# 98 units of an edge network move from a graph kernel's second layer to its third

## What is computed

```
x = norm(x + L0(x))   # softmax attention over edges
x = norm(x + L1(x))   # mean over neighbours, dense layer
x = norm(x + L2(x))   # convolution: per edge h = silu(attr10 @ W_fc1 / sqrt(10)), w = h @ W_fc2 / sqrt(100)
x = norm(x + L3(x))   # per edge w_ij = mlp(edge_feats) + mlp(chi), q * w_ij * k, weighted v
mlp(x) = silu(x @ w0 + b0) @ w1 + b1       # hidden size 256
L1: nbr_sum = segment_sum(x[row], col); aggregated = nbr_sum / clip(deg, 1)
```

## Time and profile before

| | |
|---|---|
| median of 3 runs | 8727.64 us (8727.42 to 8731.45) |
| the profiled execution | 8728.76 us, of which span 8726.9 us |
| busy: TensorE, VectorE, ScalarE, GpSimd | 83%, 69%, 60%, 38% of the span |
| mean granted TensorE clock | 0.926 of full speed |

### The profile page before, as it was taken

How to read it: one execution, slowest core, us unless ns; L and a number is a source line. 1 busy time by engine, 2 the same in 40 slices (tenths; PEclk the granted TensorE clock), 3 DMA queues, 4 the chain that set the end, 5 groups by cost and what they waited for, 6 DMA issues and landing times. The chain is left out here.

```text
span 8726.9 us, 195704 instructions
## 1 busy us (share of the span) xinstructions
PE 7226.3 (83%) x51013; PEld 5596.3 (64%) x51014; DVE 6060.3 (69%) x12581; ACT 5246.3 (60%) x9329; POOL 3328.1 (38%) x3274
## 2 busy tenths in 40 slices
PE   5999999978859999999777777777778888887775
PEld 3665666667758888888555555556556666666554
DVE  7988988989983333333666666666667777777777
ACT  3666666678856666666444444444457777776553
POOL 0000000000000000000577777777747777777776
PEclk8999999999989999999888888888889999999896
DMA  3333333366644444442222222222236666666665
GB/s 110 140 134 136 138 137 137 138 213 224 226 136 133 133 133 133 132 133 92 66 54 54 54 54 54 54 54 54 54 115 206 207 208 203 207 207 197 195 196 157
DMA packets 629186, 1179.06 MB, mean 135 GB/s; under 512 B 215307, under 2 KB 289340, under 8 KB 609685
## 3 DMA queue, kind: packets, MB, share of 16 engines
q1 hardware_dynamic: 499834, 860.28, 30.4%
q0 software_dynamic: 129280, 317.93, 13.0%
HBM read 901.19 MB, written 276.57 MB: 135 GB/s over the span
## 5 line engine op out<-in xcount | busy, mean ns | idle before, releaser
L2270 POOL DMA_INDIRECT att_kv_rows<-kv_dram,att_stage x1616 | 1624.8, 1005 | 594.8 <-issue 487.5
L2025 POOL DMA_INDIRECT conv_rows<-y_dram,conv_stage x1616 | 1635.8, 1012 | 501.0 <-issue 479.6
L1014 DVE SCALAR_TENSOR_TENSOR mean_rest<-mean_counts,mean_high 128x896 f16<-128x896 f32 x343 | 376.9, 1099 | 858.0 <-ACT mean_high L975 857.9
L695 PE MATMUL conv_part<-conv_msgs,conv_hot 128*128 128x256 f32 x3232 | 950.1, 447 | 0.0
L2003 ACT ACTIVATE conv_hid<-conv_hid_ps 100x512 f32<-100x512 f32 x408 | 221.4, 594 | 1187.3 <-PE conv_hid_ps L2034 1187.3
L695 PEld LDWEIGHTS conv_part<-conv_msgs,conv_hot 128*128 128x128 f32 x3232 | 715.7, 233 | 109.7
L1068 PE MATMUL mean_sum_ps<-wh,mean_turned 128*128 128x129 f32 x4802 | 693.4, 284 | 62.5 <-ACT mean_turned L983 62.2
L235 PE MATMUL count_ps<-count_cols,count_rows 128*128 128x392 bf16 x3920 | 729.0, 331 | 10.0 <-DVE count_cols L201 10.0
L519 PE MATMUL soft_ps<-wh,soft_weights 128*128 (+1 forms) x4802 | 580.1, 280 | 142.5 <-DVE soft_weights L463 142.5
L201 DVE TENSOR_SCALAR count_cols<-cols,col_key 128x784 bf16<-128x784 f16 x1960 | 686.2, 417 | 0.0
L2034 PE MATMUL conv_hid_ps<-conv_scalars,conv_w 10*100 10x512 f32 x816 | 280.8, 764 | 480.9 <-DMA conv_scalars<-in_scalars 479.8
(11 more groups left out here) (279 smaller groups left out, 16420.4 us busy)
## 6 DMA issues: line engine op xcount, KB each, us to landing
c_dram<-count_counts SPq DMA_DIRECT2D x392, 392.0 KB, 2.3
mean_counts<-c_dram SPq DMA_DIRECT2D x343, 448.0 KB, 3.6
att_w_rows<-w_dram SPq DMA_DIRECT2D x404, 256.0 KB
soft_counts<-c_dram SPq DMA_DIRECT2D x98, 1024.0 KB, 4.9
w_dram<-mlp_w SPq DMA_DIRECT2D x245, 256.0 KB, 2.6
soft_counts<-c_dram SPq DMA_DIRECT2D x49, 1088.0 KB, 5.0
att_lanes<-lo_dram SPq DMA_DIRECT2D x404, 128.0 KB
mlp_feats<-in_feats SPq DMA_DIRECT2D x246, 192.0 KB, 2.7
```

The source lines that it names most:

```text
L695: ins = nc.tensor.matmul(part, c.hot[:, s, t, :], rows[:, t, :], start=half == 0 and t == 0, stop=half == 1 and t == T - 1)
L1014: nc.vector.scalar_tensor_tensor(rest[:, m], counts[:, m], 0.25, high[:, m], ALU.mult, ALU.subtract).then_inc(rest_done, 1)
L2025: pool.indirect_dma_start(rows[:, s, t, :], None, y_dram, bass.IndirectOffsetOnAxis(ap=stage[:, s, t:t + 1], axis=0)).then_inc(gathered[s] ...
L2270: pool.indirect_dma_start(kv_rows[:, s, t, :], None, kv_dram, bass.IndirectOffsetOnAxis(ap=stage[:, s, t:t + 1], axis=0)).then_inc(gathere ...
```

## The change

The two units a round leave `mean_sums`. `conv_edges` takes one unit a round in its first 98 rounds (`N_CONV`), with the schedule that attention uses for one unit a round: `tensor_first` of a pair at the end of TensorE's steps 0 and 1, half of `tensor_second` at the end of steps 2 and 3, Silus at the end of ScalarE's steps 0 and 1, the bias addition after VectorE's message of the next round's step 0. To free three banks, the convolution's first layer `hid_ps` goes from two banks to one and its weights `w_ps` from four slots to two. So `first` is done for one group a step, not for two groups every second step, and `second(g + 2)` waits for the message of group `g`, not of `g - 1`. One `EdgeMlp` object lives from begin to end; the second one, with its loads in `conv_nodes`, is gone. Attention's units are the same 159.

```
-        mlp.psum(nc, st, "mean")
-                        if m in (1, 5):
-                            mlp.load_next(sp, u + m // 5)
-                        if m == 5:
-                            mlp.store(sp, u)
-                    mlp.store(sp, u + 1)
-                        first_layer(u, 2 * m - 1)
-                        first_layer(u, 2 * m)
-                        if m == 4:
-                            mlp.vector(nc, dve, u)
-                    mlp.vector(nc, dve, u + 1)
-                        units(u, 2 * m)
-                        units(u, 2 * m + 1)
...
-        hid_ps = st.enter_context(nc.psum_tensor("conv_hid_ps", [P, 2, GE], f32))
-        w_ps = st.enter_context(nc.psum_tensor("conv_w_ps", [P, S, T, D], f32))
+        hid_ps = st.enter_context(nc.psum_tensor("conv_hid_ps", [P, GE], f32))
+        w_ps = st.enter_context(nc.psum_tensor("conv_w_ps", [P, 2, T, D], f32))
+        mlp.psum(nc, st, "conv")
...
+                    if unit:
+                        mlp.sync_body(sp, U_CONV + i, 1, first)
...
+                def body(i, unit):
+                    for s in range(S):
+                        lane_hot(nc, act, c, s, S * i + s)
+
+                        act.wait_ge(w_done, S * i + s + 1)
+                        silu(S * (i + 1) + s, s)
+                        if unit:
+                            mlp.scalar_step(nc, act, U_CONV + i, s, 1)
...
-                        if s % 2 == 0:
-
-                            pe.wait_ge(hid_done, g + 4)
-                            first(s // 2, i + 2)
-
-                        pe.wait_ge(msg_done, 1 + g)
+
+                        pe.wait_ge(hid_done, g + 4)
+                        first(s, i + 2)
+
+                        pe.wait_ge(msg_done, 1 + g + 1)
                         second(g + 2, (s + 2) % S)
-                        pe.wait_ge(msg_done, 1 + g + 1)
                         lane_sums(nc, pe, c, s, g, 2 * i + s // 2, msgs[:, s])
...
+                        if unit:
+                            mlp.tensor_step(nc, pe, U_CONV + i, s, 1)
...
+                        if unit:
+                            mlp.vector_step(nc, dve, U_CONV + i, s, 1, first)
```

More of the change, by code:

```diff
@@ L760, with __init__ @@
     NC = HID // P
-    def __init__(self, nc, st, a, w_dram, label, start):
+    def __init__(self, nc, st, a, w_dram, label):
         def sb(name, shape, dt=f32):
@@ L1234, in in_order, with mean_nodes @@
         late(b)
-def mean_nodes(nc, shared, first, ident, x, wh, acc, tmp, stat, degree, node_scale, mlp, units, y_rows):
+def mean_nodes(nc, shared, first, ident, x, wh, acc, tmp, stat, degree, node_scale, y_rows):
     with ExitStack() as st:
@@ L1392, in _, with conv_nodes @@
                         add_direct(n - 4)
-def conv_nodes(nc, shared, second, ident, x, acc, sums, q_parts, node_scale, late, kv_rows):
+def conv_nodes(nc, shared, second, ident, x, acc, sums, q_parts, node_scale, kv_rows):
     with ExitStack() as st:
@@ L1427, in _ @@
             def _(sp):
-                late.begin_sync(sp)
                 for b in range(NB):
@@ L1984, in _, with body @@
                     load_scalars(p, 2 * p)
-                with sp.Fori(0, NI) as i:
+                def body(i, unit, first):
                     for s in range(S):
@@ L2030, in _, with first @@
             def _(pe):
-                def first(p, count):
-                    pe.wait_ge(scalars_in[p], 32 * count)
-                    for n in range(2):
-                        nc.tensor.matmul(hid_ps[0:100, n], w1[rows_of(n)], scalars[rows_of(n), p, :], start=True, stop=True).then_inc(hid_sum, 1)
+                def first(s, count):
+                    pe.wait_ge(scalars_in[s // 2], 32 * count)
+                    n = s % 2
+                    nc.tensor.matmul(hid_ps[0:100], w1[rows_of(n)], scalars[rows_of(n), s // 2, :], start=True, stop=True).then_inc(hid_sum, 1)
                 def second(g, s):
@@ L2038, in second @@
                     for t in range(T):
-                        ins = nc.tensor.matmul(w_ps[:, s, t, :], hid[:, s, t * P:(t + 1) * P], w2[:], start=True, stop=True)
+                        ins = nc.tensor.matmul(w_ps[:, s % 2, t, :], hid[:, s, t * P:(t + 1) * P], w2[:], start=True, stop=True)
                     ins.then_inc(w_done, 1)
                 tensor_lane_start(pe, c)
-                first(0, 1)
-                pe.wait_ge(hid_done, 2)
-                first(1, 1)
+                for s in range(S):
+                    if s > 0:
+                        pe.wait_ge(hid_done, s)
+                    first(s, 1)
                 second(0, 0)
@@ L2105, in add, with body @@
                     lane_add(nc, dve, c, s, S * i + s, k, Reach(dve, spans, k))
-                def body(i, first):
+                def body(i, first, unit):
                     for s in range(S):
@@ L2136, in attention_edges @@
         twos, ones = 63, 96
-        units = 2 * twos + ones - twos
-        assert mlp.start + units == NG
+        assert U_ATT + 2 * twos + ones - twos == NG
         def unit_of(i, per):
-            return 2 * i if per == 2 else i + twos
+            return U_ATT + (2 * i if per == 2 else i + twos)
         kv_rows = sb("kv_rows", [P, S, T, 2 * D])
@@ L2438, in _ @@
                     body(i, False, False, 1)
-                mlp.vector(nc, dve, units - 1)
+                mlp.vector(nc, dve, NG - 1)
                 with dve.Fori(ones, NI - 1) as i:
```

101 lines of the change are left out of this document (43 added, 58 removed).

## The result

The changed kernel takes 8354.02 us (median of 4 runs, 8348.42 to 8355.27) against 8729.55 us for the kernel before on the same chip: a ratio of 0.9568, 95% interval 0.9552 to 0.9585. The forecast was 8344 us. The profiled execution took 8353.9 us, with a span of 8352.1 us.

The account below looks back on a forecast made before the run. The prediction took TensorE to bound the mean layer and GpSimd to pace the convolution at 21.09 us a round. 8728.8 - 632 + 248 = 8345 us profiled, 8344 us as the median; range 8170 to 8480.

Parts of the forecast that it names:

- The mean layer: Mean layer without units: TensorE stays the bound, a round falls from 31.10 to 18.2 us, 632 us back.
- lower bound (17.6 us): Mean round if the last 0.10 us of the three products belongs to the following pair's entry; gives 662 us.
- The seam's 0.4 us: Between mean rounds: of TensorE's 1.23 us wait, 0.4 us stay once the table loads vanish.
- The units' way through the convolution: Convolution with units: TensorE waits for ScalarE's one-hot matrix behind the Silus; a round takes 23.6 us, +248 us.
- The wait: Convolution steps 1 and 2: TensorE gets the one-hot matrix 3.38 us after the unit's pair ends, arriving itself at 2.0.
- Single first layers: Convolution: one `first` a step costs 1.03 us plus 0.10 entry, partly a tiling mode change; 0.86 by columns alone.
- The clock: Convolution with units: taken as full, from attention, which waits 1.4 us and reads 1.00.
- rival of a low clock: Convolution's clock does not rise; at a mean of 0.75 a round takes 29.2 us, +795, 8891 us; chance 0.04.
- Costs of nothing: Convolution: VectorE, SyncE, GpSimd's waiting for rows, the unit's transfers and removed `conv_nodes` loads were costed at nothing.
- The unit is hidden: Rival: the convolution round stays at GpSimd's 21.1 to 22 us, 8096 to 8190 us; chance 0.15.
- chained waits: Rival: more waits chain up in the convolution, 25 to 27 us a round, 8478 to 8675 us; chance 0.12.
- a bound by loads: Rival: mean layer bound by its loads at 24.3 us a round, only 333 us back, 8643 us; chance 0.04.

Follow-up runs that it names:

- matrix-first kernel: The changed kernel with ScalarE making the next step's one-hot matrix before the unit's two Silus in the convolution: 8075.62 us, ratio 0.925.
- the one with more activations: The changed kernel with two more 128x128 activations on ScalarE behind the unit's Silus in convolution steps 0 and 1: 8490.27 us, ratio 0.9731.
- the bias kernel: The changed kernel with VectorE adding a unit's bias behind the message of step 1 instead of step 0's in the convolution: 8351.36 us, ratio 0.9566.
- banks kernel: The kernel before with the changed kernel's banks and order in `conv_edges`, its units still in `mean_sums`: 8726.15 us, ratio 0.9997.
- mean-layer-alone kernel: The changed kernel with the 98 units left out altogether, attention reading other weight blocks: 9298.65 us on the second chip, 8065.26 us on the third.
- with the seam moved: The changed kernel with SyncE's last-unit store behind the next round's loads and VectorE's bias addition behind its step 1: 9805.59 us second chip, 8342.74 us third.
- all three edits: The changed kernel with matrix ahead of the Silus, bias addition later and seam moved: 9483.65 us on the second chip, 8072.6 us on the third.

## Why the prediction was right, step by step

- **The mean layer** (forecast -632 us). Measured by rounds: 48 x (31.10 - 17.54) = 651, and 12.2 us by the first round's take, which comes at 2595.7 instead of 2607.9: 663. The mechanism was right, the term too small by 31 us. The chunk is 2.45 us, not 2.55: the pitch of 0.82 us for three products held 0.10 us of entry into the unit's pair behind it; here the same three take 0.72. The text had this as its lower bound (17.6 us) and took the other value, though the pair behind the 0.82 is exactly what the change removes. The seam's 0.4 us held. Inside the layer the memory traffic is 183 GB/s, which is seven count loads in 17.54 us (176 was reckoned for 18.2), and from 2600 to 3430 us no engine waited for a load.
- **The units' way through the convolution** (forecast 4.9, 6.3, 6.9 and 5.5 us a round, 23.6 in all; +248 us). Measured 4.9, 6.22, 7.02 and 5.63, 23.77 in all. The wait, expected to end 3.38 us behind the pair, ends at 3.23 and 3.31. Half a second layer costs 1.88 us up to the next `first`, not 1.79, and lane sums that begin after a wait take 0.10 more, as the 1.83 from 4712.54 to 4714.37 shows. The nine falls of the clock add 0.14 us on average: 84 steps of the changed kernel, from 4604.3 to 5106.4, make 23.91 us a round. Over 98 rounds that is 98 x (23.91 - 21.09) = 276, and the seam adds 10. The last three rounds have no unit but rows that were fetched ahead; eight of their steps come 3.84 to 4.06 us apart (5934.00, 5937.85), not 5.27, which is 11 of the remaining 13 us that come back. Together 273.
- **The seam** is the step that was missing. The text counted SyncE's wait at the end of a round, but not that the last unit has no round with a unit behind it in which to be stored.
- **Single first layers** were taken at 1.03 us each with 0.10 on the way in: 4703.01 to 4704.04 is 1.03. At the 0.86 of the columns alone the matrix-first kernel's round would be 0.7 us shorter than its 21.07. The Trainium skill (TensorEngine Tiling (Array Packing), Tiling Modes) states that a change of tiling mode drains TensorE; the trace agrees with a cost behind each single one, but no run separates a drain from another cost of that size. TensorE's own work was summed to 20.9; it is 21.07, since the half second layer takes 1.88 us and not 1.79, twice a round.
- **The clock** was taken as full and is 0.99. It falls to half about once in 12 rounds of the changed kernel (nine in 98), and in 39 of 98 rounds of the one with more activations, whose waits of 1.5 us are only 0.4 longer. The text had taken full clock from attention, which waits 1.4 us at a time and reads 1.00; that did not carry over to waits of 1.05 and 1.13 us here, and it cost 13 us in all. The Trainium skill (TensorE: Matmul & The Clock Gate, A second HAM failure mode: psum-queue depth-cycling) states that short idle times between groups of matmuls can make the clock fall and rise again; the trace agrees, and with the waits gone the matrix-first kernel reads 1.00 from 3700 to 5500 us. The forecast's rival of a low clock needed a mean of 0.81 or less; 0.99 is far from it.
- **Costs of nothing**: VectorE, GpSimd and SyncE inside the loop were right. GpSimd waits for messages, as foretold, and this costs nothing: the bias kernel cuts the wait by 36 us and takes the same time.
- **What is left.** Mean -663, convolution +273, and 15 us more elsewhere give the profiled -375. Of those 15, 6.2 lie between the mean layer's last take and the convolution's first step (4100.6 to 4226.0 before, 3437.7 to 3569.3 now). The banks kernel has 5.3 of them (4100.9 to 4231.6), so they belong to the banks and the order of `first`. In attention, whose program is the same, the first to the last L2397 take 5.4 us longer than before (6091.4 to 8306.7, against 6471.7 to 8681.6). Another 3.3 lie between the convolution's last step and attention's first (6351.2 to 6471.7 before, 5967.6 to 6091.4 now). What causes these last two stays open.
- **The rivals.** *The unit is hidden* is not how this kernel goes, but one moved call makes it so. It stood at 8096 to 8190 us; the matrix-first kernel takes 8076, below that range because the mean layer gives 31 us more. The wait that decided against it was not TensorE's to give or take, only a place in ScalarE's program. Neither chained waits nor a bound by loads showed up.

The sum came within 10 us, but from errors of both signs: the mean layer gave 31 us more than forecast; the convolution cost 25 more, seam and last rounds included, and the other stages 15, in all 9 us to the slow side. The mechanisms of both stages were right; that the sum comes so close is luck, since these errors have no cause in common.

## What to carry to other kernels

Where work is put into an engine's free time, look not only at that engine's sum but at each in-order program that feeds it: here TensorE's 21.1 us fitted under GpSimd's 21.1, and the round still grew by 2.8 us, because ScalarE did the new work before what the next step wanted. What waits for the end of a step belongs behind what the next step needs. And where a loop that stores its work one round late ends, the wait for the last store stands bare (10 us here): put the next loop's first loads ahead of it.

## What the chip showed beside it

Two of the three chips give the same time for one kernel within 0.1% (8729, 8722 us), the other 14% more (9959 us). The traces of the mean-layer-alone kernel on both tell where. The mean layer is as fast on either (2595.1 to 3437.0 on the slower chip, 17.54 us a round), and only the stages that gather by indirect DMA are longer: from its first to its last step the convolution takes 2597.1 us against 2111.6, attention 2960.3 against 2217.6. GpSimd's gathers of the convolution, with what they waited for, on the slower chip and then on the third:

```profile
L1989 POOL DMA_INDIRECT conv_rows<-y_dram,conv_stage x1616 | 1575.2, 975 | 1030.6 <-DVE conv_msgs L2057 552.8 <-issue 477.8
```

```profile
L1989 POOL DMA_INDIRECT conv_rows<-y_dram,conv_stage x1616 | 1626.9, 1007 | 500.4 <-issue 481.9 <-DVE conv_msgs L2057 17.1 <-DMA conv_stage<-in_src_tiles 1.5
```

Issuing a gather takes no longer on the slower chip (mean 975 and 1007 ns), and the gaps between are alike (478 and 482 us in all). What differs is that GpSimd waits for rows to come free, 552.8 us against 17.1. Slower landing of the gathers is not what the traces show: by the times of its packets a gather's last one ends 1.23 us after the issue on either chip (medians of 1616), and the packets of the gathers' queue (q0) took 12.3% of 9296.9 us there and 14.1% of 8066.8 us here, 1143 and 1137 us. VectorE's message begins 0.55 us behind the last packet of its group on the third chip and 13.7 us behind it on the slower one (medians). The rows lie ready there, and VectorE and ScalarE stand for something else; their waits on the slower chip, 4000 to 5500 us:

```profile
ACT conv_hid L1966 <- DMA y_dram<-mean_nodes_both: 646.0, 80, 16.4
DVE conv_scaled L2052 <- remote: 378.2, 63, 10.2
```

The load named in the first was done before the stage began, and the second names nothing, so what held them stays open. For the change it matters: with the seam moved the ratio on that chip is 0.9835, not 0.9563, since the units' price in the convolution, 9805.59 - 9298.65 = 507 us, is nearly twice that of the third chip, 8342.74 - 8065.26 = 277 us. The changed kernel as it is was not timed there.

A gather's mean duration in the convolution also moved with the program: 1014 ns before (4500 to 6000 us), 968 in the changed kernel, 970 with the matrix first and 1012 with all three edits (each 3700 to 5500 us), while the gaps stayed at 0.30 us. No run here says why.
